# A graph network's first layer: gathers that add onto the edges, and comparisons with their integer row in PSUM

## What is computed

```python
m = relu(node_feat[src] + edge_feat)                 # layer 0, 400000 x 32
neigh = segment_sum(m, dst, num_segments=12500)
y = (1.0 + eps[0]) * node_feat + neigh
x = layernorm(x + y)

out_deg = clip(segment_sum(ones, src), 1.0)          # layer 1
in_deg  = clip(segment_sum(ones, dst), 1.0)
agg = segment_sum((x * rsqrt(out_deg))[src], dst)
x = layernorm(x + agg * rsqrt(in_deg))
```

## Time and profile before

| | us |
|---|---|
| median of 2 runs | 6590.77 (6587.71 to 6593.83) |
| the profiled execution | 6585.29 |
| its span, from the first instruction to the last | 6583.5 |
| of the span: set-up until the first gather | 9.96 |
| first layer's groups | 4748.82 |
| first layer's norm | 60.96 |
| second layer and its norm | 1763.66 |

### The profile page before, as it was taken

One profiled execution on the slowest core, in us unless ns is written; L12 is line 12 of the kernel. 1 busy time (PEld: TensorE's weight loads), 2 busy tenths in 40 slices (PEclk: granted clock), 3 DMA queues, 4 the chain that ended last, 5 costly groups with the idle time before them and its releaser, 6 DMA issues. The chain is left out here.

```text
span 6583.5 us, 68332 instructions
## 1 busy us (share of the span) xinstructions
PE 2745.2 (42%) x22843; PEld 2292.8 (35%) x22843; DVE 2819.4 (43%) x4668; ACT 1588.2 (24%) x2158; POOL 5088.2 (77%) x4335
## 2 busy tenths in 40 slices
PE   2222222222222222222222222222358888888887
PEld 2222222222222222222222222222347676666665
DVE  5233232232232232332232332332367777777776
ACT  0000000000000000000000000000068888888885
POOL 7787787787787787787787787787767777777773
PEclk7555555555555555655555655655679999999998
DMA  2111111111111111111111111111111111111111
GB/s 45 24 21 22 24 21 21 24 21 21 24 21 22 24 21 22 24 21 22 24 21 22 24 21 22 24 21 22 18 38 19 19 19 18 19 18 19 18 19 28
DMA packets 246365, 147.86 MB, mean 22 GB/s; under 512 B 159963, under 2 KB 229164, under 8 KB 245804
## 3 DMA queue, kind: packets, MB, share of 16 engines
q0 software_dynamic: 138400, 80.97, 9.0%
q1 hardware_dynamic: 107940, 66.58, 4.1%
HBM read 141.61 MB, written 5.61 MB: 22 GB/s over the span
## 5 line engine op out<-in xcount | busy, mean ns | idle before, releaser
L133 POOL DMA_INDIRECT rows<-in_x,src_t x3125 | 3796.8, 1215 | 957.6 <-issue 952.0
L380 PE MATMUL agg<-dst_hot,msg 128*33 128x128 f32 x6250 | 943.4, 326 | 2487.5 <-ACT msg L364 2487.5
L380 PEld LDWEIGHTS agg<-dst_hot,msg 128*33 128x33 f32 x6250 | 831.2, 136 | 2593.4 <-ACT msg L364 2514.5
L133 POOL DMA_INDIRECT rows<-table,src x1200 | 1279.1, 1066 | 387.2 <-issue 377.5
L578 ACT ACTIVATE counts<-built 128x686 bf16<-128x686 f32 x1925 | 1452.8, 984 | 261.8 <-PE built L603 252.0
L364 ACT ACTIVATE msg<-edge_t 128x800 f32<-128x800 f32 (+1 forms) x126 | 108.9, 864 | 4602.8 <-DVE edge_t L297 4602.8
L297 DVE TENSOR_TENSOR edge_t<-edge_t,rows 128x800 f32<-128x800 f32 (+1 forms) x126 | 125.5, 996 | 2109.0 <-DMA rows<-in_x,src_t 2109.0
L603 PE MATMUL built<-key_hot,hi_hot 128*128 128x343 bf16 x3850 | 930.5, 325 | 103.5 <-ACT counts L578 56.7
L622 PE MATMUL applied<-counts,x_parts 128*96 128x175 bf16 x7546 | 913.7, 246 | 0.9 <-ACT prod L583 0.9
L622 PEld LDWEIGHTS applied<-counts,x_parts 128*96 128x96 bf16 x7546 | 786.3, 128 | 152.9 <-ACT counts L578 1.0
L376 PE MATMUL hist<-lo_hot,hi_hot 128*128 128x98 bf16 x3125 | 277.8, 283 | 1003.5 <-DVE lo_hot L288 1003.5
(11 more groups left out here) (109 smaller groups left out, 702.6 us busy)
## 6 DMA issues: line engine op xcount, KB each, us to landing
edge_t<-in_edge_attr SPq DMA_DIRECT2D x125, 400.0 KB
rows<-in_x,src_t POOLq DMA_INDIRECT x3125, 2.4
rows<-table,src POOLq DMA_INDIRECT x1200
src_t<-in_src SPq DMA_DIRECT2D x125, 12.5 KB
dst_t<-in_dst SPq DMA_DIRECT2D x125, 12.5 KB
base_t<-in_dst SPq DMA_DIRECT2D x125, 0.5 KB
x<-x SPq DMA_DIRECT2D x1, 1568.0 KB
x<-in_x SPq DMA_DIRECT2D x1, 1372.0 KB
```

Source lines behind the costliest of these rows:

```text
L133: gp.indirect_dma_start(rows_d[:, j, :], None, nodes, bass.IndirectOffsetOnAxis(ap=src_d[:, j:j + 1].bitcast(U32), axis=0),).then_inc(s, 16)
L380: last = te.matmul(agg[:, :], msg[:, j, :], dst_hot[:, j, :], start=(j == 0), stop=(j == J - 1))
```

## The change

The gathers of the first layer no longer write `rows`; `rows` is gone there. They get `compute_op=ALU.add` and aim at `edge_t`, so that the DMA engines add the rows of `x` onto the edges that the load has put there. VectorE's add L297 is left out, VectorE's instructions per group are 9 instead of 10, and ScalarE waits for the gathers (`s_rows`, `s_late`) and for the aggregate before.

The three comparisons read the integer row from a PSUM tensor `iota_ps`, into which VectorE copies `iota` once.

The other waits follow from that: SP waits for VectorE's fourth instruction of the group (the last that reads `src_t`) and for ScalarE before it refills; `s_agg` starts at 1; TensorE waits for `dst_hot` (`v0 + 7`) before the products with `msg`. The slow path is changed in the same way.

```diff
-        def gathers(gp, j0, j1, nodes, rows_d, src_d, s):
+        def gathers(gp, j0, j1, nodes, rows_d, src_d, s, **how):
             for j in range(j0, j1):
                 gp.indirect_dma_start(
                     rows_d[:, j, :], None, nodes,
-                    bass.IndirectOffsetOnAxis(ap=src_d[:, j:j + 1].bitcast(U32), axis=0),
+                    bass.IndirectOffsetOnAxis(ap=src_d[:, j:j + 1].bitcast(U32), axis=0), **how,
                 ).then_inc(s, 16)
...
-                rows = sb("rows", [P, 2, J, D])
...
+                iota_ps = pb("iota_ps")[:, 0:P]
+
+                s_refill = sem("s_refill")
+                VG = 9
...
                     V(ve.memset(x_0[:, :, :], 0.0))
+                    V(ve.tensor_copy(iota_ps, iota[:, :]))
...
-                            ve.tensor_tensor(hi_hot[:, :, :], tiles_of(iota[:, :], J), last_dim(s_hi[:, :], P), ALU.is_equal).then_inc(s_v, 1)
+                            ve.tensor_tensor(hi_hot[:, :, :], tiles_of(iota_ps, J), last_dim(s_hi[:, :], P), ALU.is_equal).then_inc(s_v, 1)
                             ve.wait_ge(s_v, v + 4)
-                            ve.tensor_tensor(lo_hot[:, :, :], tiles_of(iota[:, :], J)[:, :, 0:C], last_dim(s_lo[:, :], C), ALU.is_equal).then_inc(s_v, 1)
-                            ve.tensor_tensor(dst_hot[:, :, :], tiles_of(iota[:, :], J), last_dim(rel[:, :], W), ALU.is_equal).then_inc(s_v, 1)
-                            for j0, j1 in PIECES if is_last else [(0, J)]:
-                                if j0 == 0:
-
-                                    ve.wait_ge(s_rows[slot], i * (16 * J) + 16 * j1)
-                                else:
-                                    ve.wait_ge(s_late, 16 * (j1 - j0))
-                                piece = edge_t[:, slot, j0:j1, :]
-                                ve.tensor_tensor(piece, piece, rows[:, slot, j0:j1, :], ALU.add).then_inc(s_v, 1)
-                            ve.wait_ge(s_agg, g + 1)
+                            ve.tensor_tensor(lo_hot[:, :, :], tiles_of(iota_ps, J)[:, :, 0:C], last_dim(s_lo[:, :], C), ALU.is_equal).then_inc(s_v, 1)
+                            ve.tensor_tensor(dst_hot[:, :, :], tiles_of(iota_ps, J), last_dim(rel[:, :], W), ALU.is_equal).then_inc(s_v, 1)
+                            ve.wait_ge(s_agg, g + 2)
...
                         def refill(i, slot, g):
+                            sp.wait_ge(s_v, g * VG + (v0 + 4))
+                            sp.sem_inc(s_refill, 1)
                             sp.wait_ge(s_a, g + (len(ROUNDS) + 1))
                             load(g + 2, slot)
...
-                            gathers(gp, 0, n, x[:, :], rows[:, slot, :, :], src_t[:, slot, :], s_rows[slot])
+                            gathers(gp, 0, n, x[:, :], edge_t[:, slot, :, :], src_t[:, slot, :], s_rows[slot], compute_op=ALU.add)
...
-                            for n, (j0, j1) in enumerate(PIECES if isinstance(g, int) else [(0, J)]):
-                                sc.wait_ge(s_v, g * VG + (v0 + 8 + n))
+                            for j0, j1 in PIECES if isinstance(g, int) else [(0, J)]:
+
+                                if j0 == 0:
+                                    sc.wait_ge(s_rows[slot], i * (16 * J) + 16 * j1)
+                                else:
+                                    sc.wait_ge(s_late, 16 * (j1 - j0))
+                                if j0 == 0:
+
+                                    sc.wait_ge(s_agg, g + 1)
                                 sc.activation(msg[:, j0:j1, 0:D], edge_t[:, slot, j0:j1, :], ACT.Relu).then_inc(s_a, 1)
...
                     def _(te):
+                        te.sem_inc(s_agg, 1)
...
+                            te.wait_ge(s_v, g * VG + (v0 + 7))
                             for n, (j0, j1) in enumerate(PIECES if isinstance(g, int) else [(0, J)]):
```

More of the change, by code:

```diff
@@ L213, in layer_0 @@
                 misc = pb("misc")
-                VG = 10
+                iota_ps = pb("iota_ps")[:, 0:P]
+                s_refill = sem("s_refill")
+                VG = 9
                 PIECES = [(0, J - CH), (J - CH, J)]
@@ L275, in step @@
                             v = g * VG + v0
-                            is_last = isinstance(g, int)
                             ve.wait_ge(s_in[slot], (i + 1) * 64)
@@ L302, in _ @@
                         both(ve, step)
-                        V.n += VG * G + len(PIECES) - 1
+                        V.n += VG * G
                         ve.wait_ge(s_v, V.n)
@@ L348, in step @@
                             n = PIECES[0][1] if isinstance(g, int) else J
-                            gathers(gp, 0, n, x[:, :], rows[:, slot, :, :], src_t[:, slot, :], s_rows[slot])
+                            gathers(gp, 0, n, x[:, :], edge_t[:, slot, :, :], src_t[:, slot, :], s_rows[slot], compute_op=ALU.add)
                             if n < J:
-                                gathers(gp, n, J, x[:, :], rows[:, slot, :, :], src_t[:, slot, :], s_late)
+                                gathers(gp, n, J, x[:, :], edge_t[:, slot, :, :], src_t[:, slot, :], s_late, compute_op=ALU.add)
                         both(gp, step)
@@ L385, in layer_0 @@
                 A.n += G + len(PIECES) - 1
-                general_sums(0, x[:, :], J, DE, (src_t, dst_t, rows, rel, dst_hot, agg), edge_t, msg)
+                general_sums(0, x[:, :], J, DE, (src_t, dst_t, edge_t, rel, dst_hot, agg), msg)
         n_keys = n_bad = v0 = 0
@@ L640, in _, with general_sums @@
                         PE(te.matmul(small[0:1, 0:1], outside[:, :], ones[:, :], start=True, stop=True))
-                general_sums(1, table[:, :], CH, D3, (src_t, dst_t, rows, rel, dst_hot, agg), None, None)
-        def general_sums(layer, nodes, n, M, buffers, edge_t, msg):
+                general_sums(1, table[:, :], CH, D3, (src_t, dst_t, rows, rel, dst_hot, agg), None)
+        def general_sums(layer, nodes, n, M, buffers, msg):
             groups = E // (n * P)
@@ L652, in general_sums @@
             v0 = V.n
-            g_in, g_rows, g_v, g_a, g_pe = (sem(f"g_{what}{layer}") for what in ("in", "rows", "v", "a", "pe"))
-            B = 2 if layer == 0 else 1
+            g_in, g_rows, g_v, g_a, g_pe, g_mark = (sem(f"g_{what}{layer}") for what in ("in", "rows", "v", "a", "pe", "mark"))
+            B = 1
+            how = {"compute_op": ALU.add} if layer == 0 else {}
             IN = 48 if layer == 0 else 32
@@ L672, in _ @@
                             if layer == 0:
-                                load_edges(sp, g, edge_t[:, 0, :, :], g_in)
+                                load_edges(sp, g, rows[:, 0, :, :], g_in)
                 @block.gpsimd
@@ L680, in _ @@
                             gp.sem_inc(s_mark, 1)
-                            gathers(gp, 0, n, nodes, rows[:, 0, :, :], src_t[:, 0, :], g_rows)
+                            gathers(gp, 0, n, nodes, rows[:, 0, :, :], src_t[:, 0, :], g_rows, **how)
                 @block.vector
@@ L690, in _ @@
                             ve.tensor_copy(rel[:, 0:n], dst_t[:, 0, 0:n]).then_inc(g_v, 1)
-                            if layer == 0:
-                                ve.wait_ge(g_rows, (g + 1) * (16 * n))
-                                ve.tensor_tensor(edge_t[:, 0, :, :], edge_t[:, 0, :, :], rows[:, 0, :, :], ALU.add).then_inc(g_v, 1)
                             with ve.Fori(0, C) as w:
@@ L708, in _ @@
                             with sc.Fori(0, groups) as g:
-                                sc.wait_ge(g_v, g * VT + 3)
-                                sc.activation(msg[:, :, 0:D], edge_t[:, 0, :, :], ACT.Relu).then_inc(g_a, 1)
+                                sc.wait_ge(g_rows, (g + 1) * (16 * n))
+                                sc.sem_inc(g_mark, 1)
+                                sc.wait_ge(g_v, g * VT + 1)
+                                sc.activation(msg[:, :, 0:D], rows[:, 0, :, :], ACT.Relu).then_inc(g_a, 1)
                 @block.tensor
```

## The result

The changed kernel takes 7637.01 us (median of 2 runs, 7635.13 to 7638.88), the kernel before 6590.77 us: ratio 1.1587, 95% interval 1.1538 to 1.1637. The forecast was 5753 us. What came is rival C, a gather that costs GpSimd over 0.31 us more when it adds.

The account below looks back on a forecast made before the run. GpSimd's issue of the first layer's gathers was taken as the bound. 6585.3 us less 837.5 us of delays, adding free, gives 5747.8; with 5.5 us to the median, 5753 us, range 5735 to 6740.

Parts of the forecast that it names:

- rival C: First-layer gathers: adding costs over 0.31 us more each, so the kernel is slower, 7228 to 8703 us; chance 0.19.
- What bounds the kernel: First layer's 125 groups: GpSimd's issue of the gathers fills the 4748.82 us stretch, and only it moves the time.
- What the delays cost (837.5 us): First-layer gathers: time beyond 0.944 us each, without the set-up's slow ones, is removable delay, 6.70 us per group.
- Not two inputs but two SBUF inputs: Gathers beside VectorE: only instructions reading two SBUF tensors make GpSimd wait; one PSUM input does not.
- The comparisons keep their time, the cover holds: Three comparisons: no change with a PSUM input, some 5.95 us of delay a group goes, some 10.8 us cover left.
- The add leaves VectorE for nothing, no new wait: L297 and its 0.77 us delay per group go; ScalarE's and other new waits count 0, at most 24 us.
- The DMA engines: Gathers' DMA work: 0.125 us each every 1.25 us, can grow tenfold before it binds, so no cost taken.
- The gather adds. GpSimd's issue ... I take +0: GpSimd's issue of each adding gather: no extra cost, between bounds of 0.94 and 1.89 us; break-even 0.268 us.
- half as much again: Rival C's smaller price for each adding gather's issue: +0.472 us, giving 7228 us.
- A: Adding gathers cost a little more to issue, +0.03 to 0.225 us each: 5847 to 6456 us; chance 0.13.
- B: Adding gathers' issue costs about the gain, +0.225 to 0.31 us each: 6456 to 6722 us, no verdict; chance 0.04.
- D: Comparisons go on holding GpSimd despite the PSUM row; only L297's delay goes, 94 us: 6497 us; chance 0.04.

Follow-up runs that it names:

- the add from PSUM: Kernel before with the integer row in PSUM, plain gathers, and ScalarE copying gathered rows to two PSUM banks that VectorE adds: 5747.03 us, ratio 0.8724.
- the second experiment: Changed kernel with adding gathers kept but the comparisons' integer row back in SBUF: 8241.32 us, ratio 1.2506 against the kernel before.
- five adding gathers: Kernel before with the integer row in PSUM and 5 of each group's 25 gathers adding onto the edges: 6162.79 us, ratio 0.9355.

## Why the prediction was wrong

*What bounds the kernel:* right. GpSimd's issue was the bound and stayed it; the kernel after and every kernel timed against the one before moved by what its gathers' group moved.

*What the delays cost (837.5 us):* right. With the add from PSUM the time fell by 840 us from the same chip's 6587.0. How it is divided was a little off: 761 us for the comparisons, where 744 were meant, and 75 for the add instead of 94, which in a sixth of the groups holds nobody.

*"Not two inputs but two SBUF inputs":* right, but the row of L300 at 2000.72 was no evidence for it. Its gather starts 0.04 us behind VectorE's instruction, and gathers so close behind the two-SBUF add L297 weren't held either (the pair above). The 1.18 us that it should have taken when held is 1.06 by the tails of 0.82 us, which leaves a smaller gap to its 0.95. The proof is the experiment with the integer row alone.

*The comparisons keep their time, the cover holds:* right, 3491, 2700 and 3480 ns on average for the three after. *The add leaves VectorE for nothing, no new wait:* right, the gap before a gather is all "issue" as before. *The DMA engines:* right that they don't bind; their work grew 2.4 times, not ten.

*"The gather adds. GpSimd's issue ... I take +0":* **this is the step that failed.** It took the equal minimum of 128-byte and 192-byte gathers as a sign that a gather's price is set by its number of indices alone. Those rows differ in bytes; they are the same kind of instruction. From one kind they told nothing about another, and the experiment with 64-byte rows shows it: bytes don't matter to the adding gather either, at 1545 ns, and yet it is dear. The true price, +0.602 us, lay inside the bounds I had set (0 and 0.944), a little above the estimate of half as much again. With it the sum closes: 5753 + 3125 x 0.602 = 7634 us, measured 7637. Rival C named the place, the decision point (0.31) and the range of price, and had been given a chance of 0.19. The break-even was at 0.268 us, less than a third of the way between the bounds, and I had let the row nearest in number of indices outweigh that.

*Rivals:* A and B fall with the measured price, D with the integer row alone. C's second place, the DMA engines, falls with the 64-byte rows and their idle share.

The Trainium skill's pages gave the direction for C, in that an add takes two streams (DMA: Bandwidth & Descriptors, "SDMA does more than copy"). The runs agree that adding costs where casting doesn't. A third descriptor per row would however be a price per index, and four fifths of the surcharge (480 of 602 ns) are there with a quarter of the indices. What GpSimd does in that time the traces don't show; that stays open.

## What to carry to other kernels

Before an add is moved into a DMA, price the instruction that issues it on the engine that issues it; here the add cost VectorE 1 us in 38 us in which it had room, and cost the busiest engine 0.6 us 25 times. When some of GpSimd's indirect DMAs take 2 to 4 times their usual span, look for a VectorE instruction that ends one DMA's work earlier and reads two SBUF tensors; here moving one operand to PSUM, even by a copy on an idle ScalarE, removed the hold. A change in two parts wants each part's own price: of these one gained 761 us and the other cost 1881 (3125 x 0.602), and the total alone would have condemned both.

## What the runs showed that I had not expected

- An adding indirect DMA costs GpSimd 1347 / 1417 / 1546 ns at 32 / 64 / 128 indices, a plain one 867 / 907 / 944: four fifths and more of either is there with 32 indices.
- A gather that casts f32 to bf16 costs no more to issue than a plain one (937 to 941 ns against 944), though it makes 144 packets instead of 32.
- Only a gather that starts under the VectorE instruction, more than 0.045 us behind its start, is held, and not one under way: in the second experiment the one from 2024.49 took 1.54 us although `hi_hot` began at 2025.20. What a DMA's length does to the phase can thus remove a hold, as with five adding gathers.
